# Spreading the routing weights with 128-row instead of 64-row matmuls

## The reference

```
logits = einsum('th,eh->te', x, gate_weight)            # 32 experts
probs = softmax(logits);  top_val, top_idx = top_k(probs, 8)
top_val = top_val / sum(top_val)
onehot = one_hot(merge_groups[top_idx], 8)
w_tg = einsum('tk,tkg->tg', top_val, onehot)            # weight of each of 8 groups
h = einsum('th,goh->tgo', x, gate_up_proj[dominant_experts])
act = silu(gate) * up                                   # 96 values for each group
y = einsum('tgi,ghi->tgh', act, down_proj[dominant_experts])
out = einsum('tg,tgh->th', w_tg, y)
```

## Time and profile before

| | |
|---|---|
| three runs, us | 1091.14, 1093.27, 1098.48 |
| median, us | 1093.27 |
| profiled execution, first to last instruction, us | 1091.3 |
| PE busy, us (share) | 1030.8 (94%) |
| DVE busy, us (share) | 771.3 (71%) |
| ACT, POOL busy, us | 401.1, 412.5 |
| share of PE in the chain that ended last | 81% |
| mean granted PE clock | 0.985 |

### The profile page before, as it was taken

The page is one execution under the profiler, slowest core; times in us unless marked ns, Lnnn a source line. Parts: engine busy times, 40 slices in busy tenths (PEclk is TensorE's granted clock), DMA queues, the critical chain, the costliest instruction groups (busy, mean ns, idle before and its releaser), DMA issues.

```text
span 1091.3 us, 24853 instructions
## 1 busy us (share of the span) xinstructions
PE 1030.8 (94%) x9783; PEld 736.0 (67%) x9783; DVE 771.3 (71%) x1516; ACT 401.1 (37%) x723; POOL 412.5 (38%) x349
## 2 busy tenths in 40 slices
PE   5979989999899999999899998999999998999888
PEld 4546667766677667776677666766767766776566
DVE  6767688585967868677785859678695777866354
ACT  4324533254314443145331643135431443415310
POOL 1525442264505443055432634144440644316200
PEclk9989999999999999999999999999999999999999
DMA  6220000200002000200002000020001000010000
GB/s 192 59 88 2 2 1 1 68 2 2 1 2 69 2 1 1 69 2 2 1 1 70 2 2 1 1 70 1 2 1 51 19 2 1 1 49 2 2 1 20
DMA packets 22232, 23.59 MB, mean 22 GB/s; under 512 B 6314, under 2 KB 20138, under 8 KB 22130
## 3 DMA queue, kind: packets, MB, share of 16 engines
q1 hardware_dynamic: 22130, 22.02, 6.7%
HBM read 17.80 MB, written 4.21 MB: 20 GB/s over the span
## 4 chain that ended last, share of the span: by engine, by line
PE 81%; DVE 12%; issue 4%; ACT 2%; POOL 1%; DMA 1%; DVEq 0%; POOLq 0%; SPq 0%; ACTq 0%
PE ring L1138 17%; PE ring L988 12%; PE ring L989 10%; PE ring L990 10%; PE ring L1215 8%; PE av L1154 7%; PE ring L1114 6%; PE ring L1105 3%; DVE mcol L870 2%; DVE xr L909 2%; PE ring L1122 1%; PE ring L1204 1%; DVE prod L846 1%; PE av L1167 1%; PE ring L1049 1%
## 5 line engine op out<-in xcount | busy, mean ns | idle before, releaser
L679 ACT ACTIVATE pt<-ring 128x384 f32<-128x384 f32 (+1 forms) x384 | 170.8, 532 | 326.4 <-PE ring L1138 289.8
L569 POOL TENSOR_SCALAR_AFFINE_SELECT pt<-pt 128x512 f32<-128x512 f32 x128 | 79.4, 636 | 409.9 <-ACT pt L679 409.9
L870 DVE TENSOR_REDUCE mcol<-ring 128x1 f32<-128x128 f32 (+3 forms) x512 | 212.1, 481 | 19.2 <-PE ring L1114 16.8
L846 DVE TENSOR_TENSOR prod<-ring,table 128x1024 f32<-128x1024 f32 x128 | 155.2, 1217 | 93.3 <-PE ring L990 92.6
L1138 PE MATMUL ring<-rows 32*128 32x512 f32 (+3 forms) x3072 | 175.8, 330 | 9.5 <-ACT pt L679 4.9
L1138 PEld LDWEIGHTS ring<-rows 32*128 32x128 f32 x3072 | 130.7, 184 | 60.3 <-issue 35.0
L560 POOL TENSOR_TENSOR rows<-prod,rows 128x1024 fp32r<-128x1024 f32 x64 | 152.6, 2393 | 37.1 <-ACT rows L659 37.1
L553 POOL TENSOR_TENSOR prod<-prod 128x512 f32<-128x512 f32 x64 | 82.5, 1289 | 133.8 <-DVE prod L846 133.3
L659 ACT ACTIVATE rows<-prod 128x1024 fp32r<-128x1024 f32 x64 | 67.0, 1060 | 60.2 <-PE ring L1138 39.3
L1154 PE MATMUL av<-pt,vals 128*17 128x512 f32 (+3 forms) x1024 | 84.7, 436 | 1.2 <-POOL pt L569 1.2
L1138 PE MATMUL ring<-cont 32*128 32x512 f32 (+3 forms) x1024 | 85.7, 319 | 0.0
(11 more groups left out here) (164 smaller groups left out, 1633.9 us busy)
## 6 DMA issues: line engine op xcount, KB each, us to landing
xn<-x_dram SPq DMA_DIRECT2D x8, 512.0 KB, 4.3
xr<-x_dram SPq DMA_DIRECT2D x8, 512.0 KB, 4.3
out_dram<-xr SPq DMA_DIRECT2D x8, 512.0 KB, 3.2
gate_bc<-gates_scratch SPq DMA_DIRECT2D x8, 256.0 KB, 4.4
pt<-wmod_dram SPq DMA_DIRECT2D x1, 1536.0 KB, 6.3
pt<-gup_t_dram SPq DMA_DIRECT2D x16, 96.0 KB, 2.6
dn<-wu_t_dram SPq DMA_DIRECT2D x1, 640.0 KB, 9.9
xr<-wk_t_dram SPq DMA_DIRECT2D x1, 512.0 KB, 7.9
```

The lines of the kernel that those rows point to most:

```text
L679: sc.activation(pt[:, PT_AT[n] + h * w:PT_AT[n] + (h + 1) * w], ps[:, 0:w], ACT.Exp, scale=SCALE).then_inc(exp_ready.sem, 1)
L846: ve.tensor_tensor(prod[:, s % PROD, :, :], ps[:, :].unsqueeze(1).broadcast_to([P, 2, S]), table[:, :, :], ALU.mult).then_inc(rotated.sem, 1)
L870: last = ve.reduce_max(mcol[:, q, h * HR + HD:h * HR + HD + 1], ps[:, at:at + (q + 1) * P], AX_X)
```

## The change

`spread` and `wT` are allocated with 128 partitions in place of 64; in setup, DVE clears rows 64 to 127 of both once; the `weigh` matmul, whose line is unchanged, takes the whole of both operands and so is 128 rows deep. The writer of `spread` is limited to rows 0 to 63, which it wrote before. `wT` rows 0 to 63 are written per batch as before.

```
-        spread = sb("spread", [2 * NX, G * FI], F32R)
+        spread = sb("spread", [P, G * FI], F32R)
...
-        wT = sb("wT", [2 * NX, S], F32R)
+        wT = sb("wT", [P, S], F32R)
...
             ve.memset(wuk_l0[CKV:P, :].bitcast(F32), 0.0)
+            ve.memset(spread[2 * NX:P, :].bitcast(F32), 0.0)
+            ve.memset(wT[2 * NX:P, :].bitcast(F32), 0.0)
             ve.memset(wuv_l0[CKV:P, :].bitcast(F32), 0.0)
...
-                        ve.tensor_scalar(spread[:, :].rearrange("p (g i) -> p g i", g=G),
+                        ve.tensor_scalar(spread[0:2 * NX, :].rearrange("p (g i) -> p g i", g=G),
```

## The result

The changed kernel takes 1080.55 us (median of 6 runs, 1076.42 to 1086.63) beside 1095.8 for the kernel before in the same rounds: a ratio of 0.9859, 95% interval 0.9814 to 0.9904. The forecast was 1082.5 with a range of 1078.7 to 1088.6, and from the median of the first three runs (1093.27) a gain of 10.8; 15.3 was measured between these medians. The profiled execution has a span of 1075.2 where that of before had 1091.3: 16.1 less. The time of an execution is 1.9 to 2.2 us longer than its span in every run on record (1077.32 and 1075.2 here), so the span of before belongs to a time near the median of its three runs, 1093.3, and not to the fastest.

What follows compares the result with a forecast made beforehand. PE, busy 94% of the span, was taken as the bound. Switches 9.3 plus clock 1.5 minus clearings 0 gave 10.8 us, from the 1093.27 median to 1082.5 us; range 1078.7 to 1088.6.

Steps and rivals of the forecast that it cites:

- What bounds the kernel, and what the gap is: PE bounds the kernel; around `weigh`, changing between 128 and 64 rows leaves 0.36 us gaps, whatever the operands.
- The switches removed: Row-count changes around three `weigh` groups per batch: 0.39 us each, 1.17 per batch, 9.3 us gained over eight batches.
- The 128-row price: A 128-row `weigh` matmul was taken to cost the projection's 0.234 us, against 0.23 for the 64-row one.
- the two passes: Rival: wide `weigh` takes two passes over its columns, 0.234 us more in each of 48, 1095.2 us; chance 0.03.
- exposed loads: Rival: `weigh` weight loads no longer run under the matmul before, costing 7.2 of the 9.3, 1091.2 us; chance 0.03.
- one side only: Rival: only the way into or out of the `weigh` groups gets cheaper, half the gain, 1088.6 us; chance 0.05.
- Passed on to the end: PE reaches `down` 1.17 us earlier, DVE moves along by 0.78, nothing becomes late, and the whole gain carries through.
- The clearings: Two DVE clearings in setup, 0.48 + 0.73 = 1.2 us once, costed at nothing because DVE idles 4.69 us afterwards.
- The clock: Clock falls after the mix stage in batches 0, 2, 4, 6: two of four expected to go, 1.5 us gained.
- runs that agree with the span: Runs matching the profiled span of 1091.3 us; with three or four falls gone, given 0.36 on the faster side.
- the lower baseline of the range: The range's fast end: all four clock falls gone, counted from the span, 1091.1 - 12.4 = 1078.7 us.
- The rhythm: Clock falls begin 256.0 us apart, two batches take 256.07; batches shorter by 1.17 us no longer fit that.

Runs made afterwards that it cites:

- the kernels without falls in the loop: Changed kernel and kernel before, each with six added matmuls per batch where PE waits in the mix stage; 1078.0 and 1087.8 us.
- restored length: Changed kernel with five more 128-row `weigh` matmuls per batch, ahead of `weigh` 03, results overwritten; 1092.4 us, ratio 0.998.

## Why the prediction was right, and where it was off

**What bounds the kernel, and what the gap is:** right. The gap goes with the row count: 128-row and 96-row `weigh` don't have it, 64-row matmuls of other operands do, and each group pays for itself.

**The switches removed:** right in size. Forecast 1.17 a batch and 9.3 in all; the profile gives 1.15 to 1.18 for batches free of falls, the kernels without falls in the loop 9.8 between medians. The Trainium skill, "TensorEngine Tiling (Array Packing)", Key Properties, says that a change of tiling mode drains the array; the trace agrees that a change of row count from 128 to 64 costs something and puts 0.39 us on it there and back, while no run shows that a drain is what fills the gap. The advice of the same page of the Trainium skill (When to Use Tiling) to tile for 64 rows, weighed in the prediction, had nothing to give here: no second `weigh` ran beside the first, and the steps of one, two and three in the earlier trace rows grew by 0.23 each.

**The 128-row price:** taken as the projection's 0.234, measured 0.23. The rivals of the two passes, of exposed loads and of one side only fall with the first chain after the change, and with them the rule of the Trainium skill, "TensorE: Matmul & The Clock Gate", The mechanism (Part 3), that a load overlaps running matmuls only on other row groups, by which the loads would have come into the open: at 306.55 and 306.79 they run under the 128-row matmuls before them.

**Passed on to the end:** right. DVE's idle time before `up.05`'s product was to shrink by 0.78 and shrank from 1.03 to 0.26; `down` met no wait.

**The clearings:** right, at nothing; the spread one took 0.70 where 0.73 was estimated.

**The clock:** the mis-sized term. "I take two of four, 1.5 us" was too little, and its bounds were drawn round the wrong set. In the profiled execution all four falls of the mix stages went (3.2), with one in the last batch (0.8) and what the falls of setup cost more before (2.7), which the sum didn't have. The step that failed was to read one execution's falls as the kernel's. Over 44 executions of the kernel before in the later rounds the granted clock goes from 0.971 to 0.993, mean 0.984, times 1088.1 to 1104.6; in the ten of the changed kernel it goes from 0.983 to 0.998, mean 0.9905. Time falls as the clock rises, along much the same line in both, 6.5 to 7 us for 0.01, so the mean difference of 0.0068 is some 4 to 5 us. Straight lines fitted to the two sets lie 9.0 apart at an equal clock of 0.987, which is the switches again. The slowest executions of the kernel before (1102.5 to 1104.6) have a clock of 0.971 to 0.973, as has the profile with the restored length, in which every batch has a fall twice as long; that it is the same in the kernel before is likely, but no profile of such an execution was kept.

**The total:** near the forecast in part by luck. The gain between medians was 4.5 us larger than forecast; 2.5 of that is the baseline, which was 1093.27 for the first three executions and 1095.8 for six, and 2.0 the changed kernel. Between the means of the 44 and the ten it is 13.7: the 9.3 of the switches and the clock's 4 to 5. The chance given to "runs that agree with the span" and the lower baseline of the range rest on setting the span beside the fastest run, where by the record it belongs to the median.

**The rhythm:** not shown. The changed kernel has on average fewer falls than the kernel before. But the kernel with the restored length owes its old time mainly to its five added matmuls (9.4 of 11.0 us), five of seven stages had falls with 96 rows and batches of the same short length, and the clocks of the restored kernel (mean 0.9858 in ten) overlap with the changed one's. That the falls of the loop need PE's waiting in the mix stage is shown, since matmuls in those gaps removed them in both kernels without changing the length of a batch; how far their number follows the length of a batch, and why the changed kernel has fewer, stays open.

## What to carry to other kernels

Where a few 64-row matmuls stand among 128-row ones, and nothing else uses the rest of the rows beside them (where something does, nothing was tried here), pad both operands with zero rows: a matmul of 512 columns took 0.23 us at either height, and each stretch of them saved 0.39 us, for 1.2 us of clearing once that lay in idle time. Read such a price from start to start on either side of the odd matmul: its own listed duration shows only part of it (0.50 us beside 0.39), and no wait on a semaphore shows it. And when a kernel's runs differ by more than the change is worth, compare at equal granted clock, or fill the waits of PE so that the clock stays up, before a term for it is put into a sum.

## What was not expected of the hardware

A kernel that repeats a stretch in which PE waits can settle into falls of the clock in every second batch (256.0 us apart for two batches in the profile of before) or into longer ones in every batch (129.7 us apart, 1100.9 us in all, with the length restored). Six matmuls in a batch, put where PE waits, took these falls away and left the looped batches of a profile within 0.1 us of each other. And a matmul of 96 rows among 128-row ones costs no change, while one of 64 does.
